# Quantised tokens taken from the low half word of a rounding constant, in a fused wavelet, attention and feed-forward layer

## The reference, cut to what matters

```
_act_quant(x):  scale = 127 / clip(max|x| over the row, 1e-5);  round(x*scale) / scale
h = h + attention(layernorm(h))
h = h + bitlinear(silu(bitlinear(y, w_gate)) * bitlinear(y, w_up), w_down),  y = layernorm(h)
bitlinear(x, w) = act_quant(x) @ ternary(w)^T
layernorm(x) = (x - mean) / sqrt(var + 1e-5)
```

## Time and profile before

| | |
|---|---|
| median of 3 runs | 2324.99 us (2322.57 to 2325.19) |
| the profiled execution | 2319.44 us, its span 2317.6 us |
| mean granted TensorE clock | 0.946 |
| busy: TensorE, VectorE, ScalarE, GpSimd | 79%, 69%, 59%, 51% of the span |
| one step in the steady part | some 65 us (residual sum L1144 at 998.35 and again at 1063.43 us) |
| chain that ended last | TensorE 37%, VectorE 36%, issue 12%, ScalarE 11% |

### The profile page before, as it was taken

One profiled execution on the slowest core, in us unless ns is written; L12 is line 12 of the kernel. 1 busy time (PEld: TensorE's weight loads), 2 busy tenths in 40 slices (PEclk: granted clock), 3 DMA queues, 4 the chain that ended last, 5 costly groups with the idle time before them and its releaser, 6 DMA issues.

```text
span 2317.6 us, 48979 instructions
## 1 busy us (share of the span) xinstructions
PE 1821.9 (79%) x16742; PEld 1316.3 (57%) x16742; DVE 1604.3 (69%) x4832; ACT 1357.1 (59%) x3841; POOL 1176.6 (51%) x1290
## 2 busy tenths in 40 slices
PE   2656888788888888888888888888888888888775
PEld 1634665556665655565565665556665665555553
DVE  2435767776777777777777777777767767777765
ACT  0124666666666666666666666666666666666653
POOL 0136555566555555566555554566555555565500
PEclk6769999999999999999999999999999999999986
DMA  7312111112111111111111211112211111111100
GB/s 188 132 27 51 43 42 47 37 47 51 51 45 44 47 42 45 39 48 51 51 48 41 51 39 44 37 49 51 52 46 44 49 39 45 43 43 45 47 10 10
DMA packets 98073, 113.74 MB, mean 49 GB/s; under 512 B 22721, under 2 KB 60066, under 8 KB 97570
## 3 DMA queue, kind: packets, MB, share of 16 engines
q1 hardware_dynamic: 97826, 110.61, 18.5%
HBM read 26.62 MB, written 8.42 MB: 15 GB/s over the span
## 4 chain that ended last, share of the span: by engine, by line
PE 37%; DVE 36%; issue 12%; ACT 11%; SPq 2%; POOL 1%; DMA 0%; DVEq 0%; ACTq 0%; POOLq 0%
PE bank L614 16%; DVE arena L1045 5%; PE bank L764 4%; DVE ptr_l L1050 4%; DVE arena L1197 4%; DVE es L1200 4%; DVE th L1193 4%; PE bank L848 3%; PE bank L704 3%; PE bank L716 2%; ACT arena L499 2%; DVE arena L1160 2%; PE bank L702 2%; DVE ao L1069 2%; PE bank L725 2%
## 5 line engine op out<-in xcount | busy, mean ns | idle before, releaser
L465 POOL TENSOR_TENSOR arena<-rq,cos 128x256 f32<-128x256 f32 (+1 forms) x384 | 345.5, 915 | 584.0 <-ACT rq L491 584.0
L499 ACT ACTIVATE arena<-arena,nm 128x129 f32<-128x129 f32 (+1 forms) x1024 | 458.2, 457 | 34.0 <-DVE nm L1045 33.9
L470 POOL TENSOR_TENSOR rot<-rot,sin 128x512 f32<-128x512 f32 x256 | 338.4, 1322 | 231.0 <-DMA rot<-rq 230.8
L1045 DVE CUSTOM_DVE_ANT_0 arena<-bank,bias 128x129 f32<-128x129 f32 (+1 forms) x1024 | 305.3, 353 | 179.7 <-PE bank L704 171.9
L1050 DVE TENSOR_TENSOR ptr_l<-bank,ptr_h 128x384 f16<-128x384 f32 x512 | 281.7, 550 | 182.4 <-ACT ptr_h L504 181.9
L614 PE MATMUL bank<-xt_h,weights 128*128 128x256 f16 x2048 | 385.1, 276 | 20.7 <-ACT rq L491 17.4
L614 PE MATMUL bank<-arena,ptr_h 128*128 128x64 f16 x3072 | 208.7, 195 | 213.0 <-DVE ptr_l L1050 110.3
L491 ACT ACTIVATE rq<-bank,bqk 128x256 f32<-128x256 f32 x512 | 214.3, 470 | 261.0 <-PE bank L614 250.1
L504 ACT ACTIVATE ptr_h<-bank 128x384 f16<-128x384 f32 x512 | 250.3, 489 | 195.0 <-PE bank L716 194.6
L474 POOL TENSOR_TENSOR arena<-arena,rot 128x256 f32<-128x256 f32 (+1 forms) x384 | 331.6, 878 | 37.6 <-POOL rot L470 1.4
L614 PEld LDWEIGHTS bank<-arena,ptr_h 128*128 128x128 f16 x3072 | 179.3, 99 | 260.0 <-DVE ptr_l L1050 254.9
(11 more groups left out here) (186 smaller groups left out, 3398.2 us busy)
## 6 DMA issues: line engine op xcount, KB each, us to landing
rot<-rq SPq DMA_DIRECT2D x1024, 64.0 KB, 2.0
arena<-in_x SPq DMA_DIRECT2D x4, 2048.0 KB, 18.2
xin<-in_x SPq DMA_DIRECT2D x32, 256.0 KB, 2.7
hr<-hr SPq DMA_DIRECT2D x32, 256.0 KB, 2.4
out<-h SPq DMA_DIRECT2D x64, 128.0 KB, 1.7
arena<-in_L_attn_w_qkv SPq DMA_DIRECT2D x2, 1536.0 KB, 6.4
arena<-in_L_attn_w_out SPq DMA_DIRECT2D x1, 1024.0 KB, 10.1
arena<-in_L_ffn_w_gate SPq DMA_DIRECT2D x1, 1024.0 KB, 6.4
```

The costliest lines, as they stand in the source:

```text
L465: ins = pool.tensor_tensor(dst, rq[:, g % 2, :, cols], cos[:, cols].unsqueeze(1).broadcast_to([P, 2, cols.stop - cols.start]), ALU.mult)
L470: pool.tensor_tensor(r, r, sin[:, :].unsqueeze(1).broadcast_to([P, 2, SIDE]), ALU.mult).then_inc(t2_ready, 1)
L499: act.activation(cols, cols, ACT.Exp, bias=nm[:, t, h:h + 1], scale=-1.0, accum_out=rs[:, t, h:h + 1]).then_inc(e_done, 1)
L1045: dve.tensor_tensor_reduce(r[:, cols], bank[:, cols], b, -1.0, 3.0e38, ALU.add, ALU.min, nm[:, t, h:h + 1]).then_inc(t_done, 1)
```

## The change

Four things. **Rounding constant**: the constant added is now MAGIC + 0x6600, whose sum with a whole number n has the float16 number 1536 + n in its low half word. The second pass that took the constant off again (ScalarE's `xq`, VectorE's `q2`) is gone: `xq` and `q2` are views with a stride of two half words on the float32 tile, TensorE transposes those, and the copies out of PSUM (`xqt`, `q2t`) take 1536 off by a bias. **Tokens**: they are centred but not scaled, by a `tensor_scalar` with an accumulator output (its sum is used by nobody), and this and the search for the largest value stand in slot 4, ahead of `pt_lo` and `normalise`; slot 5 keeps only the scales. **Scales**: operations on two columns are now two operations on one column, `rstd2` enters in the scales. **Inner activations**: `gu` has one buffer per half of the tokens, and the first half's part of the largest value is scaled at once.

```
+HALF_ZERO = 1536.0
+ROUND = MAGIC + 0x6600
-        gu = carve(INNER)
+        gu = [carve(INNER) for _ in range(T)]
+        xq = th[:, 0, :].bitcast(F16)[:, 0::2].rearrange("p (t n) -> p t n", t=T)
+        q2 = [half.bitcast(F16)[:, 0::2] for half in gu]
...
-                        act.activation(q2t[...], g_bank[:, :].bitcast(F16), ACT.Copy).then_inc(q2t_done, 1)
+                        identity(q2t[...], g_bank[:, :].bitcast(F16), bias=half_zero[:, 0:1]).then_inc(q2t_done, 1)
-                        act.activation(xqt[...], u_bank[:, 0:SIDE].bitcast(F16), ACT.Copy).then_inc(xqt_done, 1)
+                        identity(xqt[...], u_bank[:, 0:SIDE].bitcast(F16), bias=half_zero[:, 0:1]).then_inc(xqt_done, 1)
...
                         for t in range(T):
-                            ins = identity(xn2[:, t, :], xn2[:, t, :], bias=magic[:, 0:1], scale=es[:, 4 + t:5 + t])
-                        ins.then_inc(xround_done, 1)
-                        act.wait_ge(xround_done, e + 1)
-                        identity(xq[:, :, :], xn2[:, :, :], bias=neg_magic[:, 0:1]).then_inc(xq_ready, 1)
+                            ins = identity(xn2[:, t, :], xn2[:, t, :], bias=round_to[:, 0:1], scale=es[:, 4 + t:5 + t])
+                        ins.then_inc(xq_ready, 1)
...
-                        pe.wait_ge(q2_ready, 2 * e + t + 1)
+                        pe.wait_ge(round_done, 2 * e + t + 1)
...
-            def quantise_tokens(e, ep):
+            def centre_tokens(ep):
-                dve.wait_ge(rstd2_ready, e + 1)
                 for t in range(T):
-                    ce.mark(ts(xn2[:, t, :], h2[:, ep, t, :], mv2[:, t, 0:1], rstd2[:, t:t + 1], ALU.subtract, ALU.mult))
+                    ce.mark(ts(xn2[:, t, :], h2[:, ep, t, :], mv2[:, t, 0:1], 0.0, ALU.subtract, ALU.max, accum_out=es[:, 8 + t:9 + t]))
                 ce.settle()
                 ce.link(dve.tensor_reduce(es[:, 0:2], xn2[:, :, :], AX.X, ALU.max, apply_absolute_value=True))
-                ce.link(ts(es[:, 0:2], es[:, 0:2], 1e-5, None, ALU.max))
+            def token_scales(e):
+                dve.wait_ge(rstd2_ready, e + 1)
+                for t in range(T):
+                    ce.mark(ts(es[:, t:t + 1], es[:, t:t + 1], rstd2[:, t:t + 1], 1e-5, ALU.mult, ALU.max))
+                ce.settle()
                 ce.link(dve.reciprocal(es[:, 2:4], es[:, 0:2]))
-                ce.mark(ts(es[:, 6:8], es[:, 0:2], wsc[:, 9:10], None, ALU.mult))
-                ce.link(ts(es[:, 8:10], es[:, 0:2], wsc[:, 10:11], None, ALU.mult))
-                ce.mark(tt(es[:, 10:12], es[:, 6:8], es[:, 8:10], ALU.mult))
-                ts(es[:, 4:6], es[:, 2:4], 127.0, None, ALU.mult).then_inc(tscale_ready, 1)
+                for t in range(T):
+                    ts(es[:, 4 + t:5 + t], es[:, 2 + t:3 + t], rstd2[:, t:t + 1], 127.0, ALU.mult, ALU.mult).then_inc(tscale_ready, 1)
+                for t in range(T):
+                    ts(es[:, 6 + t:7 + t], es[:, t:t + 1], wsc[:, 9:10], None, ALU.mult).then_inc(hscale_ready, 1)
+                for t in range(T):
+                    ce.mark(ts(es[:, 10 + t:11 + t], es[:, t:t + 1], es[:, t:t + 1], wsc[:, 12:13], ALU.mult, ALU.mult))
+                ce.settle()
...
-                f = es[:, 10 + t:11 + t]
-                ce.link(ts(es[:, 12 + t:13 + t], es[:, 22:23], es[:, 23:24], f, ALU.max, ALU.mult))
-                ce.link(ts(es[:, 12 + t:13 + t], es[:, 12 + t:13 + t], 1e-5, None, ALU.max))
-                ce.link(dve.reciprocal(es[:, 14 + t:15 + t], es[:, 12 + t:13 + t]))
-                ce.mark(ts(es[:, 20 + t:21 + t], es[:, 12 + t:13 + t], wsc[:, 11:12], None, ALU.mult))
-                ts(es[:, 18 + t:19 + t], es[:, 14 + t:15 + t], f, 127.0, ALU.mult, ALU.mult).then_inc(s2_ready, 1)
+                f, floor, peak = es[:, 10 + t:11 + t], es[:, 14 + t:15 + t], es[:, 12 + t:13 + t]
+                ce.link(ts(peak, es[:, 23:24], f, floor, ALU.mult, ALU.max))
+                ce.link(dve.reciprocal(es[:, 16 + t:17 + t], peak))
+                ts(es[:, 18 + t:19 + t], es[:, 16 + t:17 + t], f, 127.0, ALU.mult, ALU.mult).then_inc(s2_ready, 1)
+                ts(es[:, 20 + t:21 + t], peak, wsc[:, 11:12], None, ALU.mult).then_inc(oscale_ready, 1)
...
-                    if has_e and k - 1 in Q2_SLOT:
-                        dve.wait_ge(round_done, 2 * e + t + 1)
-                        ts(q2[:, :], gu, -MAGIC, None, ALU.add).then_inc(q2_ready, 1)
...
                         norm_stats(ce, dst, st2, mv2, ve2, var2_ready, e)
+                        centre_tokens(ep)
                     if has_e and k == XQ_SLOT:
-                        quantise_tokens(e, ep)
+                        token_scales(e)
...
+                        if n % 2 == 0:
+                            ce.mark(ts(es[:, 14 + t:15 + t], es[:, 22:23], es[:, 10 + t:11 + t], 1e-5, ALU.mult, ALU.max))
+                        else:
                             inner_scale(e, t)
```

More of the change, by code:

```diff
@@ L149, in vit_layer @@
         magic = sb("magic", [P, 1])
-        neg_magic = sb("neg_magic", [P, 1])
+        round_to = sb("round_to", [P, 1])
+        half_zero = sb("half_zero", [P, 1])
         wsc = sb("wsc", [P, 16])
@@ L532, in step @@
                             act.wait_ge(down_ready, 2 * e + t)
-                        act.activation(q2t[:, :, :].rearrange("p j n -> p (j n)"), g_bank[:, :].bitcast(F16), ACT.Copy).then_inc(q2t_done, 1)
+                        identity(q2t[:, :, :].rearrange("p j n -> p (j n)"), g_bank[:, :].bitcast(F16), bias=half_zero[:, 0:1]).then_inc(q2t_done, 1)
                     if has_e and k == XQT_SLOT:
                         act.wait_ge(xqt_ready, e + 1)
-                        act.activation(xqt[:, :, :].rearrange("p k n -> p (k n)"), u_bank[:, 0:SIDE].bitcast(F16), ACT.Copy).then_inc(xqt_done, 1)
+                        identity(xqt[:, :, :].rearrange("p k n -> p (k n)"), u_bank[:, 0:SIDE].bitcast(F16), bias=half_zero[:, 0:1]).then_inc(xqt_done, 1)
                     if has_b and k in QK_SLOT:
@@ L574, in step @@
                         act.wait_ge(s2_ready, 2 * e + t + 1)
-                        identity(gu, gu, bias=magic[:, 0:1], scale=es[:, 18 + t:19 + t]).then_inc(round_done, 1)
+                        identity(gu[t], gu[t], bias=round_to[:, 0:1], scale=es[:, 18 + t:19 + t]).then_inc(round_done, 1)
                     if has_e and k in GU_SLOT:
                         n = GU_SLOT.index(k)
+                        act.wait_ge(hscale_ready, 2 * e + n // 2 + 1)
                         act.wait_ge(g_ready, 4 * e + n + 1)
@@ L1124, in step @@
                         output(e, ep, 0)
-                    if has_e and k - 1 in Q2_SLOT:
-                        t = Q2_SLOT.index(k - 1)
-                        dve.wait_ge(round_done, 2 * e + t + 1)
-                        if not start or t == 1:
-                            dve.wait_ge(q2t_ready, 2 * e + t)
-                        ts(q2[:, :], gu, -MAGIC, None, ALU.add).then_inc(q2_ready, 1)
                     if has_e and k == H2_SLOT:
@@ L1194, in step @@
                         dve.wait_ge(gate_done, 4 * e + n + 1)
-                        if n % 2 == 0 and not (start and n == 0):
-                            dve.wait_ge(q2_ready, 2 * e + t)
-                        tt(gu[:, cols], u_bank[:, :], th[:, n % 2], ALU.mult).then_inc(gu_done, 1)
+                        if n % 2 == 0 and not start:
+                            dve.wait_ge(q2t_ready, 2 * e + t - 1)
+                        tt(gu[t][:, cols], u_bank[:, :], th[:, n % 2], ALU.mult).then_inc(gu_done, 1)
                         dve.wait_ge(gu_done, 4 * e + n + 1)
-                        ce.link(dve.tensor_reduce(es[:, 22 + n % 2:23 + n % 2], gu[:, cols], AX.X, ALU.max, apply_absolute_value=True))
-                        if n % 2 == 1:
+                        ce.link(dve.tensor_reduce(es[:, 22 + n % 2:23 + n % 2], gu[t][:, cols], AX.X, ALU.max, apply_absolute_value=True))
+                        if n % 2 == 0:
+                            ce.mark(ts(es[:, 14 + t:15 + t], es[:, 22:23], es[:, 10 + t:11 + t], 1e-5, ALU.mult, ALU.max))
+                        else:
                             inner_scale(e, t)
```

23 lines of the change are left out of this document (12 added, 11 removed).

## The result

The changed kernel takes 2338.02 us, the median of 4 runs (2335.43 to 2343.06), and the kernel before in the same comparison 2323.78 (2320.38 to 2325.19). The ratio is 1.0066 (1.0045 to 1.0087): slower by 0.66%, 14 us, where 2350 was forecast with a range of 2312 to 2376. The profiled execution took 2335.43 us, its span 2333.6 against 2317.6 before.

The account below looks back on a forecast made before the run. No engine bounds the whole step; the path `ao` - TensorE - ScalarE and VectorE's token chain arrive almost together. Delays of +5 us and the clock's +25 on the profiled 2319.4 gave 2350 us, range 2312 to 2376.

Parts of the forecast that it names:

- The delay of `ao`: Slot 4: centring and search now stand ahead of `ptr_l` and `ao`, making `ao` later by 1.55 us a step.
- The scale chain: Slot 5 on VectorE: 2.6 us less work, but only 0.07 us a step of it reaches the path.
- rival 3: What VectorE saves is saved: 4.4 us a step, 145 us in all, 2175 us; chance 3%.
- First gate product: It comes 0.84 us later a step: 1.55 - 0.07 - 0.73 for the dropped rounding pass + 0.09 for the bias.
- Slots 8 to 10: From the first to the third gate product, mainly by losing the subtraction into `q2`: -0.62 us a step.
- The copies with a bias: ScalarE's copies `xqt` and `q2t` read a bias per partition: +0.09 us each.
- The strided loads: TensorE's weight loads of `q2` and `xq` with a stride of two half words: +0.15 us a step.
- The clock: The longer slot 5 wait halves TensorE's clock in 65% of steps; with slot 12, +0.82 us a step, +25 us.
- rival 1: Delays as summed, but the clock does not fall at the new place: 2324 or 2330 us; chance 20%.
- a quieter slot 12: The wait in slot 12 shortens by some 0.18 us and the clock falls somewhat less often there: -0.25 us a step.
- Rival 2: The clock's fall at slot 12 goes and none comes: 2298 us, or 2310 if half go; chance 13%.
- rival 4: The new wait falls every time, centring waits for GpSimd, strided loads cost their 0.38 us: 2375 us; chance 14%.

Follow-up runs that it names:

- Experiment 1: The changed kernel with the centring and the search put back behind `ao`, in slot 5: 2245.20 us, ratio 0.9659 to the kernel before.
- experiment 4: The kernel before with only slot 5's two-column scale operations done one column at a time, in their old place: 2315.61 us, ratio 0.9959.
- experiment 2: The kernel before with the token part alone (centring and search ahead of `ao`, single-column scales), two-pass rounding kept: 2395.17 us, ratio 1.0311.
- kernel 8: The kernel before with `ptr_l` and `ao` of slot 4 put ahead of the residual sum and its statistics: 2419.99 us, ratio 1.0421.
- kernel 10: The kernel before with `ptr_l` and `ao` ahead of the residual sum and single-column scales in slot 5: 2324.12 us, ratio 1.0005.
- Experiment 6: The changed kernel with eight unused TensorE products added in slot 5, ahead of head 4's values: 2307.14 us, ratio 0.9933 to the kernel before.
- kernel 5: The changed kernel with the centring as a plain `tensor_scalar` without accumulator output, in its new place: 2323.65 us, ratio 1.0004 to the kernel before.
- kernel 7: The changed kernel with `ptr_l` and `ao` of slot 4 ahead of the residual sum, centring behind them: 2223.83 us, ratio 0.9573.

## Why the prediction held, step by step

**The delay of `ao`** was priced at +1.55. The mean of 28 steps went from 2.92 to 4.49, +1.57, and in steps in which nothing else holds `ao` up, from 2.67 to 4.32, +1.65. The difference is the accumulating pair, 0.87 with its reads instead of 0.77: one takes 471 ns and not the 418 of the statistics pass that stood in for it. Experiment 1 shows that this term is passed on to the gate product in full.

**The scale chain**, -0.07, was the step that kept rival 3 out. Its size was right (0.06 by experiment 4), but the pair of steps it was read from was read wrongly. ScalarE in the step of the earlier trace rows, and then in that of the earlier trace rows:

```profile
1008.37 0.41 ACT L499 ACTIVATE arena<-arena,nm 128x129 f32<-128x129 f32 x1 [0.17 <-DVE nm L1045]
```

```profile
1073.03 0.49 ACT L504 ACTIVATE ptr_h<-bank 128x384 f16<-128x384 f32 x1 [4.98 <-PE bank L716]
```

In the first step ScalarE did pause, 0.17 us for VectorE's scores, which were late because the scale chain ended 6.65 us behind `ao`. In the second it started 0.28 us later behind `ao` than in the first, after a wait that the trace puts down to TensorE. That both made 14.30 was chance. All 28 steps of that trace side by side tell it: where the chain ends at most 6.35 us behind `ao`, 14 steps, the gate product comes 14.02 to 14.04 behind `ao` (but for the step of the earlier trace rows); in the other 14, what the chain is longer is passed on, to 14.09 at 6.43, 14.31 at 6.65 and 14.42 at 6.77. The mean is 14.09, so 0.07 was there to gain. Rival 3 (2175 us) falls by experiments 4 and 2 for this order of instructions; with `ao` first its mechanism holds (kernels 8 and 10).

**First gate product**: without the clock +0.84 was predicted, and +0.84 is what the means give: +1.57 for `ao`, and from `ao` to the gate product 13.36 instead of 14.09, -0.73 against the -0.71 summed. **Slots 8 to 10**: -0.62 predicted. Steps of the usual length went from 12.49 to 11.80, -0.69; the mean, -0.82, holds 0.13 more because long steps have become rarer. In eight of the 28 steps before, the subtraction into `q2` took 1.10 us instead of 0.79 and the stretch 12.88 to 13.67. The copies with a bias cost what was said: ScalarE's groups, 500 to 2000 us, are

```profile
L495 ACT ACTIVATE q2t<-bank,half_zero 128x1024 f16<-128x1024 f16 x46 | 51.1, 1112 | 0.0
L495 ACT ACTIVATE xqt<-bank,half_zero 128x512 f16<-128x512 f16 x22 | 15.1, 687 | 12.4 <-PE bank L807 12.4
```

against 1020 and 597 before, +0.09 each.

**The strided loads** were a wrong term, and a small one. I took +0.15 from loads of four-byte elements. TensorE's loads of `q2` and `xq`:

```profile
L858 PEld LDWEIGHTS bank<-eye,arena 128*128 128x128 f16 x368 | 29.7, 117 | 2.3
L807 PEld LDWEIGHTS bank<-eye,th 128*128 128x128 f16 x88 | 5.3, 96 | 26.1 <-issue 26.1
```

117 ns against 110, and 96 for `xq` against the same 96 before. These loads come nowhere near the 142 ns of the four-byte ones; 8 x 7 ns is 0.06 us at most, and no stretch shows it.

**The clock.** I let it fall in slot 5 in 65% of the steps at 1.65 each: 57% and 1.70 were measured (gate product 13.36 behind `ao` without a fall, 15.06 with one), +0.97 a step against +1.07. That the share came so near is luck: the trace before has no wait of this length at that place, and no run shows in which steps the clock falls. Experiment 6 takes the falls of slot 5 away and gets 31 us, 0.91 a step up to the first gate product and 0.22 behind the third, with five falls fewer in slot 12. So rival 1 (2324 to 2330) falls: the new wait does throttle. The Trainium skill ("TensorE: Matmul & The Clock Gate", section "HAM oscillation — how this bites in real kernels") names this pattern, a wait in each turn of a loop with the work behind it at the lower clock. It tells it of every turn; here it came in 16 steps of 28, so these runs agree in part, and the measurement decides. The -0.25 for a quieter slot 12 did not come: 21 falls against 20, and a fall there makes the step 1.53 us longer now against 1.35 before, though the three in slot 11 went. Rival 2 falls with it. Of rival 4 (2375) nothing came: no fall in every step, no wait for GpSimd in the centring, no price on the loads.

**Sums.** The time came 12 us under the forecast and well inside the range, but the change was summed at +30 us on the profiled execution and the profiled executions differ by 16: about half. A steady step was forecast at +1.22 and lost 0.80 to 0.86; the last three at -7 and gave 7.3. By the means over 28 steps the 0.36 between 1.22 and 0.86 are: 0.10 up to the first gate product, all of it the clock; 0.20 between the first and the third (-0.82 against -0.62); and 0.07 behind (-0.14 against -0.07). The last is small by luck. In steps without a fall there, that stretch went from 34.28 to 34.07, -0.21, where +0.18 was summed (-0.06 + 0.09 + 0.15), and the falls cost 0.07 a step more where 0.25 less was forecast: two wrong terms, 0.39 and 0.32, that nearly cancel. 30 steps of 0.36 are 11 us. The mechanism up to the first gate product was right in each term; the sum behind it was too high.

## What to carry to other kernels

Before moving work ahead of an instruction, ask who waits for that instruction and what stands in order behind the waiter: three operations that cost nothing behind `ao` cost 93 us ahead of it, more than the 79 that all the rest of the change saved. A gain in an engine's work counts only where its wait ends last, and all steps of one trace side by side, sorted by where one chain ends, can tell that without a run; two steps picked from it can mislead. A path with slack turns late when the other gets early: the same single-column scales gave 9 us with `ao` behind the statistics and 96 with `ao` first. And a wait in front of dense TensorE work has a second price, the clock, to be worked out apart from the wait itself; where the wait can't go, cheap products that nobody reads can stand in it.

## What the runs showed of the hardware

- A wait of TensorE of 2.3 to 3.4 us that recurs once a step was followed by half the clock in 16 steps of 28 and not in the others, where it was 2.3 to 2.75; filler products in the wait removed all these falls (31 us). A fall cost 1.70 us here and 1.35 to 1.53 in slot 12. The number of falls in slot 12, behind the same wait of 1.9 us, was 21 with the change, 16 in kernel 6, 15 in 5, 11 in 1 and 10 in 7; what sets it no run shows.
- An accumulating `tensor_scalar` on 128x256 float32 took 471 ns, the plain one 344; the plain pair took 0.61 us where GpSimd did not hold it up, 1.26 and 2.61 beside its rotations, the accumulating pair 0.87 in both places.
- Operations on two columns took up to 1.18 us beside GpSimd's rotations, and the same work on single columns 0.14 to 0.27 each (kernels 8 and 10).
- A ScalarE copy with a bias read per partition took 90 ns longer than the plain copy at 512 columns and 92 at 1024.
- Weight loads of float16 with a stride of two half words took 0 and 7 ns more than dense ones (96 and 117 ns against 96 and 110).
